# All attention-times-V matmuls of a unit in one block of a slot, in a hand-ordered cross-attention kernel

## The chip, the cores and the metric

The kernel runs on one NeuronCore of a Trainium2 chip, in one launch. The metric is the device time of that launch in microseconds, the median of the runs shown. Five engines run their own instruction streams and meet only at semaphores: TensorE (PE; its weight loads are shown as PEld), VectorE (DVE), ScalarE (ACT), GpSimd (POOL) and SyncE (SP), which here issues all DMAs.

## The reference

Cross attention with 16 heads of width 32, a residual and a layer norm, for 8 batches of 224 queries (width 512) over 750 context tokens:

```
q = x @ Wq.T + bq; k = ctx @ Wk.T + bk; v = ctx @ Wv.T + bv      # 16 heads of 32
att = softmax(q k^T / sqrt(32)); o = att v; o = o @ Wo.T + bo
y = layernorm(x + o, eps=1e-5) * gamma + beta
```

## The kernel before, in words

**Units, steps, slots.** Four heads form a unit, so a batch has 4 units and the launch has 32 (`NU`). The whole order is written out by hand. A batch is 32 steps, in 4 groups of 8 (`UNIT`). Each engine walks the same steps in its own loop and has its own list of what is due in each. Batches 0, 6 and 7 and a last, shorter iteration 8 are written out; batches 1 to 5 are a hardware loop (`batches`, line 265).

**What a step holds.** In step s of group g TensorE first does the query-major scores of the next step's head and half of the queries: 2 matmuls of 375 keys (`scores`, line 491). VectorE takes the row maxima of them (`row_max`, line 744). They are only there to find each query's maximum; their three half banks are used in turn (`RING = 3`), and the last half of a batch is put into bank 1 (`BANK[-1] = 1`, line 73). The unit before (u−1) has its maxima turned by TensorE to the other layout in step 0 of the group (`turn_maxima`, line 504), ScalarE copies them into the operand stack (`save_maxima`, line 637), and from step 2 on each step does two pieces of key-major scores, 2 matmuls each, into two banks in turn (`scores_keymajor`, line 514), and ScalarE's exp of each (`exp`, line 644). The exps give `probsT`, keys by queries, 6 key tiles of 125 keys.

**Attend and sums.** `attend(u, g, k, batch)` (line 530) multiplies key tile k of `probsT` with V for the four heads of a unit: 4 float32 matmuls, each in its own 32 columns of the array (the trace shows 8 records). `sum_keys` (line 558) does the same with ones on `head_sums`, which POOL has added up over the key tiles, 3 instructions a head (`sum_head`, line 854). Both write `ps_attn`. After the sums ScalarE copies `ps_attn` out (`copy_attn`), VectorE inverts the sums in two halves and scales (`invert_sums`, `scale_attn`), and ScalarE and VectorE save a high and a low float16 part (`attn_high`, `attn_low`). `STAGES` (line 100) gives for each of these how many groups behind the unit's scores it comes, and in which step of that group; `due` reads it, `TAIL` is the same for iteration 8.

**Tasks.** At the end of a step TensorE may have one task: K, Q or V projections (12 matmuls each, 3 for each product of float16 parts), transposes of context or x (4), or half of the output projection O (12). They go in turn into the two banks of `ps_task`. ScalarE saves the high part one step later, then VectorE the low part (`save_task`, line 701; V has only the VectorE copy). The next task but one waits for that save (line 609). `OWN`, `NEXT` and `OUTPUT` (lines 89 to 94) say which task is in which step, for this batch, the next, and the one before.

**SyncE's order.** In each batch: fill the stacks of unit 2 (16 DMAs), move V tiles 0 to 3 from `v_next` to `v_now`, fill the stacks of unit 3, move V tiles 4 and 5, load the next inputs, fill the stacks of unit 0 of the next batch, store the outputs, load the residual, fill those of unit 1. A move may start only when the last attend with the old tile is done. In the written-out batches it waits for that attend itself; in the loop it waits for the save of the first task at or after step `LAST_USE + k` (line 399). The first unit of a batch waits for the moved tile k in its attend k (line 536).

Of the kernel before, what the change touches and what calls it, by code (L numbers as in the profile page):

```python
# [15 lines left out]
def build(nc, x, ctx_tokens, Wq, bq, Wk, bk, Wv, bv, Wo, bo, gamma, beta, out):  # L50
# [7 lines left out]
    KT = 6  # L58
# [4 lines left out]
    UNIT = 2 * HG  # L63
# [13 lines left out]
    NU = B * UNITS  # L77
# [11 lines left out]
    OWN = {0: ("K", 2, 0), 1: ("V", 0), 2: ("K", 2, 1), 3: ("Q", 2), 4: ("K", 3, 0), 5: ("V", 1), 8: ("K", 3, 1),  # L89
           9: ("V", 2), 11: ("V", 3), 12: ("Q", 3), 14: ("V", 4), 17: ("V", 5)}  # L90
    NEXT = {6: ("ctxT", 0), 10: ("ctxT", 1), 13: ("ctxT", 2), 15: ("K", 0, 0), 16: ("K", 1, 0), 18: ("ctxT", 3),
            19: ("ctxT", 4), 20: ("xT", 0), 21: ("ctxT", 5), 22: ("xT", 1), 23: ("K", 0, 1), 25: ("Q", 0),
            27: ("K", 1, 1), 29: ("Q", 1)}
    OUTPUT = {24: ("O", 0), 26: ("O", 1)}
    assert all(len(t) % 2 == 0 for t in (OWN, NEXT, OUTPUT))
    assert not OWN.keys() & NEXT.keys() and not (OWN.keys() | NEXT.keys()) & OUTPUT.keys()
    O_STEPS = sorted(OUTPUT)


    STAGES = {**{("attend", k): (2, 2 + k) for k in range(KT)}, "sum_keys": (2, 7), "copy": (3, 0), ("invert", 0): (3, 1),  # L100
              ("invert", 1): (3, 2), "scale": (3, 3), "high": (3, 4), "low": (3, 5)}
    TAIL = {NU - 3: {"copy": 0, ("invert", 0): 1, ("invert", 1): 2, "scale": 3, "high": 4, "low": 5},
            NU - 2: {**{("attend", k): max(k, 1) for k in range(KT)}, "sum_keys": 5, "copy": 6, ("invert", 0): 7, ("invert", 1): 8,
# [5 lines left out]
    assert 2 * UNIT + LOW_STEP < O_STEPS[0] and O_STEPS[1] < 3 * UNIT + HIGH_STEP  # L109
    LAST_USE = UNIT + 2  # L110
# [63 lines left out]
    with ExitStack() as stack:  # L174
# [151 lines left out]
        def _(sp):  # L326
# [50 lines left out]
            def iteration(b):  # L377
# [9 lines left out]
                if 0 in tasks:  # L387
# [4 lines left out]
                    def move(k):  # L392


                        if isinstance(b, int):
                            need(sp, attn_ready, KT * (UNITS * b - 1) + k + 1)
                            sp.wait_ge(task_saved, after(("V", k)))
                        else:
                            s = min(s for s in tasks if s >= max(STEP_OF["V", k], LAST_USE + k))
                            sp.wait_ge(task_saved, before + tasks[s][1] + 1)  # L400
                        move_v(k)
# [37 lines left out]
        def _(pe):  # L439
# [144 lines left out]
            def iteration(b):  # L584
                tasks = iteration_tasks(b)
                before = tasks_before(b)
                for s in range(STEPS):
# [4 lines left out]
                    if u is not None:  # L592
                        if s % UNIT == 0:
                            turn_maxima(u, (g - 1) % UNITS)
# [30 lines left out]
        def _(act):  # L625
# [47 lines left out]
            def iteration(b):  # L673
                tasks = iteration_tasks(b)
                before = tasks_before(b)
                for s in range(STEPS):
# [7 lines left out]
                    if u is not None:  # L684
                        if s % UNIT == 0:
                            save_maxima(u, (g - 1) % UNITS)
# [246 lines left out]
```

## Time and profile before

| | us |
|---|---|
| three runs | 739.58, 738.58, 736.05 |
| median | 738.58 |
| span of the profiled execution, first to last instruction | 737.1 |
| PE, PEld busy | 688.3, 441.4 |
| DVE, ACT, POOL busy | 515.8, 336.3, 454.9 |
| mean granted TensorE clock | 0.980 |

For the profiled execution there is only its span; no time outside it was recorded. Matmuls are pipelined and their records overlap, so the cost of a group of them is the distance from its start to the start of the next. In a timeline a row is: start, us, engine, line, operation, names, shapes, how many merged, and in brackets the idle time before it and what ended it. Times count from the span's start.

### The profile page before, as it was taken

To read this page: it belongs to the slowest core of one execution; us is meant where nothing else is said; L and a number is where in the kernel's file an instruction comes from. 1 tells how busy PE (TensorE), PEld (TensorE's weight loads), DVE (VectorE), ACT (ScalarE), POOL (GpSimd) and SP (SyncE) were. 2 spreads that over 40 slices of the span, in tenths; PEclk is the share of its full clock that TensorE was granted. 3 is DMA by queue.
4 is the path that set the end of the run, shared out by engine and by line. 5 is a ranking of instruction groups with operands and counts; after the bars stand their busy time and mean duration, and the time that the engine had idled before them with its cause. 6 is when DMAs were issued, how large, how long until landed. Compare 5 with 4: busy or idle time off the path is not lost.

```text
span 737.1 us, 16224 instructions
## 1 busy us (share of the span) xinstructions
PE 688.3 (93%) x5496; PEld 441.4 (60%) x5496; DVE 515.8 (70%) x967; ACT 336.3 (46%) x657; POOL 454.9 (62%) x458
## 2 busy tenths in 40 slices
PE   5849999999999999999999999999999999999884
PEld 4626765666656665666656665666656666566542
DVE  2626676668867588777776688666886677666796
ACT  3501464546444464445444464444545464344461
POOL 9200666665686567674587666764686756776763
PEclk8979999999999999999999999999999999999998
DMA  4843233222332332323323223323323321223110
GB/s 156 268 123 87 88 108 103 58 69 75 123 82 61 95 110 79 88 67 87 125 78 74 83 92 101 85 57 94 113 68 93 97 57 27 83 66 93 32 52 26
DMA packets 46867, 64.95 MB, mean 88 GB/s; under 512 B 14781, under 2 KB 27069, under 8 KB 46829
## 3 DMA queue, kind: packets, MB, share of 16 engines
q1 hardware_dynamic: 46829, 64.45, 30.5%
q8 instruction: 23, 0.38, 0.2%
q14 instruction: 15, 0.12, 0.1%
HBM read 24.52 MB, written 3.67 MB: 38 GB/s over the span
## 4 chain that ended last, share of the span: by engine, by line
PE 81%; DVE 8%; DMA 6%; issue 4%; SPq 1%; DVEq 0%; ACT 0%; POOL 0%
PE ps_task L487 36%; PE ps_attn L539 10%; PE ps_scores L500 10%; PE ps_scoresT L525 8%; PE ps_task L448 6%; DVE top_halves L749 4%; PE ps_task L461 3%; DMA ctx_in<-in_ctx 3%; DMA stacks<-parts 2%; PE ps_scoresT L509 2%; PE ps_attn L565 2%; PE ps_task L465 1%; DVE y L734 1%; DVE attn_parts L779 1%; DMA v_now<-v_next 1%
## 5 line engine op out<-in xcount | busy, mean ns | idle before, releaser
L749 DVE TENSOR_REDUCE top_halves<-ps_scores 112x1 f32<-112x375 f32 x512 | 253.8, 537 | 191.9 <-PE ps_scores L500 190.8
L859 POOL TENSOR_TENSOR pair_sums<-probsT 125x672 f32<-125x672 f32 x122 | 201.2, 1650 | 209.2 <-ACT probsT L651 203.3
L651 ACT ACTIVATE probsT<-ps_scoresT 125x448 f32<-125x448 f32 x384 | 187.9, 541 | 183.9 <-PE ps_scoresT L525 181.5
L500 PE MATMUL ps_scores<-stacks 96*112 96x375 f16 x512 | 131.1, 333 | 23.7 <-DMA stacks<-parts 11.8
L487 PE MATMUL ps_task<-wvT,ctxT 128*125 128x512 f16 x576 | 133.3, 381 | 0.0
L487 PE MATMUL ps_task<-ctxT,wkT 128*128 128x375 f16 x744 | 131.1, 326 | 0.0
L539 PE MATMUL ps_attn<-probsT,v_now 125*32 125x224 f32 x1488 | 109.8, 367 | 1.3 <-DMA v_now<-v_next 1.2
L525 PE MATMUL ps_scoresT<-stacks 100*125 100x224 f16 x768 | 106.8, 260 | 0.3 <-ACT stacks L640 0.2
L487 PEld LDWEIGHTS ps_task<-wvT,ctxT 128*125 128x125 f16 x576 | 76.6, 136 | 47.2 <-issue 7.5
L487 PEld LDWEIGHTS ps_task<-ctxT,wkT 128*128 128x128 f16 x744 | 68.6, 98 | 56.8 <-issue 18.4
L500 PEld LDWEIGHTS ps_scores<-stacks 96*112 96x112 f16 x512 | 62.2, 131 | 61.4 <-DVE top_halves L749 24.7
L525 PEld LDWEIGHTS ps_scoresT<-stacks 100*125 100x125 f16 x768 | 88.9, 136 | 13.3 <-ACT probsT L651 2.9
L864 POOL TENSOR_TENSOR head_sums<-pair_sums 125x224 f32<-125x224 f32 x122 | 81.7, 669 | 10.1
L867 POOL TENSOR_TENSOR head_sums<-head_sums,pair_sums 125x224 f32<-125x224 f32 x122 | 82.0, 672 | 9.6
L633 ACT ACTIVATE parts<-ps_task,bk 128x375 f16<-128x375 f32 x62 | 35.6, 575 | 109.6 <-PE ps_task L487 109.6
L762 DVE RECIPROCAL recip<-attn_sums 128x112 f32<-128x112 f32 x64 | 53.5, 840 | 1.5 <-ACT attn_sums L659 1.5
L539 PEld LDWEIGHTS ps_attn<-probsT,v_now 125*32 125x32 f32 x1488 | 29.7, 108 | 28.6 <-DMA v_now<-v_next 1.7
L448 PE MATMUL ps_task<-woT,attn_parts 128*112 128x512 f16 x192 | 44.5, 382 | 0.1
L487 PE MATMUL ps_task<-xT,wqT 128*128 128x224 f16 x384 | 42.2, 259 | 0.0
L487 PEld LDWEIGHTS ps_task<-xT,wqT 128*128 128x128 f16 x384 | 35.2, 98 | 8.4 <-issue 5.4
L711 DVE SCALAR_TENSOR_TENSOR parts<-ps_task,bk,parts 128x375 f16<-128x375 f32 x62 | 37.0, 597 | 1.7 <-ACT parts L633 1.7
L448 PEld LDWEIGHTS ps_task<-woT,attn_parts 128*112 128x112 f16 x192 | 23.7, 130 | 18.3 <-issue 4.0
(87 smaller groups left out, 588.1 us busy)
## 6 DMA issues: line engine op xcount, KB each, us to landing
stacks<-parts SPq DMA_DIRECT2D x256, 60.9 KB, 2.0
v_now<-v_next SPq DMA_DIRECT2D x48, 250.0 KB
ctx_in<-in_ctx SPq DMA_DIRECT2D x7, 1500.0 KB
stacks<-parts SPq DMA_DIRECT2D x128, 46.9 KB, 2.0
x_in<-in_x SPq DMA_DIRECT2D x8, 448.0 KB, 14.8
resid<-in_x SPq DMA_DIRECT2D x8, 448.0 KB, 4.2
out_y<-y SPq DMA_DIRECT2D x16, 224.0 KB, 2.3
stacks<-parts SPq DMA_DIRECT2D x128, 14.0 KB, 1.8
```

The costliest lines, as they stand in the source:

```text
L448: last = nc.tensor.matmul(bank[0:QP, :], attn_parts[:, a, k, QP * q:QP * q + QP], wT["o"][:, c, k, :], start=(k == 0 and (a, c) == (0, 0)) ...
L487: last = nc.tensor.matmul(dst, lhsT, rhs, start=first, stop=(n_mm == 0))
L500: nc.tensor.matmul(ps_scores[0:QP, BANK[i], 0:KH], stacks[0:STACK_ROWS, g, h, NK + QP * q:NK + QP * q + QP], stacks[0:STACK_ROWS, g, h, KH ...
L525: last = nc.tensor.matmul(ps_scoresT[0:KP, piece % 2, NQ * i:NQ * i + NQ], stacks[:, g, h, KP * k:KP * k + KP], stacks[:, g, h, Qc], start ...
L539: last = nc.tensor.matmul(ps_attn[c:c + DK, 0:NQ], v_now[0:KP, k, P * g + c:P * g + c + DK], probsT[0:KP, g % 2, h, k, :], start=(k == 0), ...
L651: nc.scalar.activation(probsT[0:KP, g % 2, h, 2 * j:2 * j + 2, :].rearrange("p k q -> p (k q)"), ps_scoresT[0:KP, piece % 2, 0:2 * NQ], AC ...
L711: nc.vector.scalar_tensor_tensor(dst, src, b16, high, ALU.add, ALU.subtract).then_inc(task_saved, 1)
L749: nc.vector.tensor_reduce(top_halves[0:QP, g % 2, q, h, c:c + 1], ps_scores[0:QP, BANK[2 * s + c], 0:KH], AX.X, ALU.max).then_inc(half_top ...
L762: nc.vector.reciprocal(recip[:, cols], attn_sums[:, 1, cols]).then_inc(recip_ready, 1)
L859: nc.gpsimd.tensor_tensor(pair_sums[0:KP], probsT[0:KP, g % 2, h, 0:3, :], probsT[0:KP, g % 2, h, 3:6, :], ALU.add).then_inc(pair_sums_rea ...
L864: nc.gpsimd.tensor_tensor(head_sums[0:KP, g % 2, h, :], pair_sums[0:KP, 0], pair_sums[0:KP, 1], ALU.add).then_inc(two_sums_ready, 1)
L867: nc.gpsimd.tensor_tensor(head_sums[0:KP, g % 2, h, :], head_sums[0:KP, g % 2, h, :], pair_sums[0:KP, 2], ALU.add).then_inc(head_sums_read ...
```

## The change

All six attends and the sums of a unit move into step 1 of the group (`VISIT = 1`), two groups behind the unit's scores, and the following stages into the rest of the same group. The turn of the next unit's maxima moves from step 0 to step 1, ahead of them. Tasks are put into other steps; their number is the same. On SyncE, the loop's wait of the V moves follows the last use, which is now the same step for every key tile.

```diff
-    OWN = {0: ("K", 2, 0), 1: ("V", 0), 2: ("K", 2, 1), 3: ("Q", 2), 4: ("K", 3, 0), 5: ("V", 1), 8: ("K", 3, 1),
-           9: ("V", 2), 11: ("V", 3), 12: ("Q", 3), 14: ("V", 4), 17: ("V", 5)}
-    NEXT = {6: ("ctxT", 0), 10: ("ctxT", 1), 13: ("ctxT", 2), 15: ("K", 0, 0), 16: ("K", 1, 0), 18: ("ctxT", 3),
-            19: ("ctxT", 4), 20: ("xT", 0), 21: ("ctxT", 5), 22: ("xT", 1), 23: ("K", 0, 1), 25: ("Q", 0),
+    OWN = {0: ("K", 2, 0), 1: ("Q", 2), 2: ("K", 2, 1), 3: ("V", 0), 4: ("K", 3, 0), 5: ("V", 1), 6: ("V", 2), 7: ("V", 3),
+           8: ("K", 3, 1), 9: ("Q", 3), 10: ("V", 4), 11: ("V", 5)}
+    NEXT = {12: ("ctxT", 0), 13: ("ctxT", 1), 14: ("ctxT", 2), 15: ("xT", 0), 16: ("K", 0, 0), 17: ("ctxT", 3),
+            18: ("K", 1, 0), 19: ("ctxT", 4), 22: ("ctxT", 5), 23: ("xT", 1), 24: ("K", 0, 1), 25: ("Q", 0),
             27: ("K", 1, 1), 29: ("Q", 1)}
-    OUTPUT = {24: ("O", 0), 26: ("O", 1)}
+    OUTPUT = {20: ("O", 0), 21: ("O", 1)}
...
-    STAGES = {**{("attend", k): (2, 2 + k) for k in range(KT)}, "sum_keys": (2, 7), "copy": (3, 0), ("invert", 0): (3, 1),
-              ("invert", 1): (3, 2), "scale": (3, 3), "high": (3, 4), "low": (3, 5)}
-    TAIL = {NU - 3: {"copy": 0, ("invert", 0): 1, ("invert", 1): 2, "scale": 3, "high": 4, "low": 5},
-            NU - 2: {**{("attend", k): max(k, 1) for k in range(KT)}, "sum_keys": 5, "copy": 6, ("invert", 0): 7, ("invert", 1): 8,
+    VISIT = 1
+    STAGES = {**{("attend", k): (2, VISIT) for k in range(KT)}, "sum_keys": (2, VISIT), "copy": (2, 2), ("invert", 0): (2, 3),
+              ("invert", 1): (2, 4), "scale": (2, 5), "high": (2, 6), "low": (2, 7)}
+    TAIL = {NU - 2: {**{("attend", k): max(k, 1) for k in range(KT)}, "sum_keys": 5, "copy": 6, ("invert", 0): 7, ("invert", 1): 8,
                      "scale": 9, "high": 10, "low": 10},
...
-    LAST_USE = UNIT + 2
+    LAST_USE = UNIT + VISIT
...
-                            s = min(s for s in tasks if s >= max(STEP_OF["V", k], LAST_USE + k))
+                            s = min(s for s in tasks if s >= max(STEP_OF["V", k], LAST_USE))
...
-                        if s % UNIT == 0:
+                        if s % UNIT == VISIT:
                             turn_maxima(u, (g - 1) % UNITS)
...
-                        if s % UNIT == 0:
+                        if s % UNIT == VISIT:
                             save_maxima(u, (g - 1) % UNITS)
```

## Rows read from the trace of the kernel before

**Rows 1.** Windows, one loop batch: PE, PEld, DVE, ACT, POOL busy, clock, DMA.
```profile
290.70:375.50 84.80, 83.34 (x677) 53.30 (x673) 62.31 (x118) 40.77 (x80) 56.60 (x59) 1.00 0.31 88
```
**Rows 2.** Waits in that window: who waited for whom, us, times, longest.
```profile
PE ps_scores L500 <- DVE top_halves L749: 1.5, 1, 1.5
```
**Rows 3.** Timeline of PE, batch 3, group 0: score pairs that begin steps.
```profile
299.68 0.49 PE L500 MATMUL ps_scores<-stacks 96*112 96x375 f16 x2
...
302.16 0.49 PE L500 MATMUL ps_scores<-stacks 96*112 96x375 f16 x2
...
305.40 0.49 PE L500 MATMUL ps_scores<-stacks 96*112 96x375 f16 x2
...
309.36 0.49 PE L500 MATMUL ps_scores<-stacks 96*112 96x375 f16 x2
```
**Rows 4.** Timeline of PE, batch 0, group 1, where no attends are due yet.
```profile
78.13 0.49 PE L500 MATMUL ps_scores<-stacks 96*112 96x375 f16 x2
...
80.00 0.49 PE L500 MATMUL ps_scores<-stacks 96*112 96x375 f16 x2
...
81.13 0.49 PE L500 MATMUL ps_scores<-stacks 96*112 96x375 f16 x2
```
**Rows 5.** Timeline of PE in the tail: attends and sums in a row.
```profile
714.87 0.58 PE L539 MATMUL ps_attn<-probsT,v_now 125*32 125x224 f32 x8
715.27 0.56 PE L565 MATMUL ps_attn<-head_sums,ones 125*32 125x224 f32 x8
...
716.53 0.31 PE L525 MATMUL ps_scoresT<-stacks 100*125 100x224 f16 x1
```
**Rows 6.** Timeline of PE around a turn of maxima.
```profile
354.68 0.49 PE L500 MATMUL ps_scores<-stacks 96*112 96x375 f16 x2
355.10 0.55 PE L509 MATMUL ps_scoresT<-ident,top 112*4 112x112 f32 x4
355.58 2.80 PE L448 MATMUL ps_task<-woT,attn_parts 128*112 128x512 f16 x12
```
**Rows 7.** Timeline of DVE in batch 3.
```profile
305.77 1.00 DVE L749 TENSOR_REDUCE top_halves<-ps_scores 112x1 f32<-112x375 f32 x2 [1.50 <-PE ps_scores L500]
...
343.28 0.68 DVE L717 COPY v_next<-ps_task 125x512 f32<-125x512 f32 x1
343.88 0.84 DVE L762 RECIPROCAL recip<-attn_sums 128x112 f32<-128x112 f32 x1
344.64 0.93 DVE L749 TENSOR_REDUCE top_halves<-ps_scores 112x1 f32<-112x375 f32 x2
345.49 0.67 DVE L713 TENSOR_TENSOR ctxT<-ps_task,ctxT 128x500 f16<-128x500 f32 x1
346.07 1.03 DVE L769 TENSOR_TENSOR attn<-attn_sums,recip 128x224 f32<-128x224 f32 x1
```
**Rows 8.** Timeline of ACT: two exps of one step.
```profile
367.61 0.98 ACT L651 ACTIVATE probsT<-ps_scoresT 125x448 f32<-125x448 f32 x2
```
**Rows 9.** Timeline of SP's issues: two DMAs into stacks, two V moves.
```profile
364.21 1.22 SPq L343 DMA_DIRECT2D stacks<-parts  x2
...
681.59 1.61 SPq L349 DMA_DIRECT2D v_now<-v_next  x2
```
**Rows 10.** The chain's last V move (start, us), and the attend behind it (PE timeline).
```profile
682.46 6.42 DMA v_now<-v_next
...
688.92 0.59 PE L539 MATMUL ps_attn<-probsT,v_now 125*32 125x224 f32 x8 [1.18 <-DMA v_now<-v_next]
```
**Rows 11.** Timeline of POOL: two heads' sums begin; a beta pass.
```profile
348.50 1.64 POOL L859 TENSOR_TENSOR pair_sums<-probsT 125x672 f32<-125x672 f32 x1
...
351.80 1.64 POOL L859 TENSOR_TENSOR pair_sums<-probsT 125x672 f32<-125x672 f32 x1
...
374.12 1.28 POOL L887 TENSOR_TENSOR y<-y,beta_row 112x512 f32<-112x512 f32 x1
```
**Rows 12.** Windows, just behind the idle at the end of batch 4.
```profile
459.00:462.00 3.00, 3.00 (x24) 1.14 (x23) 1.25 (x4) 1.51 (x3) 3.00 (x3) 0.53 0.24 72
```

More of the change, by code:

```diff
@@ L108, in build @@
     SUM_STEPS = ((1, 4, 0), (1, 5, 1), (1, 7, 2), (2, 0, 3))
-    assert 2 * UNIT + LOW_STEP < O_STEPS[0] and O_STEPS[1] < 3 * UNIT + HIGH_STEP
-    LAST_USE = UNIT + 2
+    assert UNIT + LOW_STEP < O_STEPS[0] and O_STEPS[1] < 2 * UNIT + HIGH_STEP
+    LAST_USE = UNIT + VISIT
     STEP_OF = {t: s for s, t in {**OWN, **NEXT, **OUTPUT}.items()}
```

## The prediction

> **What bounds the kernel now.** I read four views. The windows row of one batch in the loop (the fourth, 84.80 us long) says which engine is full: TensorE 83.34 us busy, VectorE 62.31, POOL 56.60, ScalarE 40.77, at a granted clock of 1.00 [rows 1]. Waits in that window: TensorE idles once, 1.5 us, for a row maximum [rows 2]. So a batch is TensorE's own stream, and a TensorE microsecond saved is real until something else is late. The timelines then give prices: TensorE's by start-to-start distances, since recorded matmuls overlap.
>
> **Prices of a step on TensorE.** Between two score pairs: a Q step takes 2.48, a K step 3.24, a V step 3.96 [rows 3]. Batch 0, group 1 has no attends yet: there the Q step takes 1.87 and a context transpose step 1.13 (80.00 to 81.13) [rows 4], against 1.80 for the latter with an attend. So one lone attend costs 0.61 to 0.67, 0.64 on average, though its 8 recorded matmuls in a row need 0.38. Bare parts: scores 0.33, two key tiles 0.38, and the task: K 1.92, V 2.59, Q 1.16, O 2.64, transpose 0.44.
>
> **What the block saves.** The tail shows column-tiled groups back to back: 714.87, 715.27, then two more, and the next full-array load at 716.53 [rows 5]. Hence first 0.40, each middle one (716.53 − 0.50 − 715.27) / 2 = 0.38, last with exit 0.50. Seven groups (six attends, the sums): 0.40 + 5 × 0.38 + 0.50 = 2.80. The turn costs 0.48 with its exit and 0.09 to enter (0.42 instead of 0.33) [rows 6]. Turn to attend is not in the trace. Bounds: 0 (no switch at all; less is excluded, the four columns' matmuls still take their turn) to 0.26, all that a lone attend pays for entering and leaving; I take the nearest row, the turn's own entry, 0.09. Scores + turn + block = 0.42 + 0.38 + 0.09 + 2.80 = 3.69. A unit now pays 6 × 0.64 + 0.38 + 0.57 = 4.8, afterwards 3.36: 1.4 less, 5.7 a batch.
>
> The Trainium skill, "TensorEngine Tiling (Array Packing)", Key Properties, says that changing the tiling mode, not merely the tile, drains TensorE. The lone attend's 0.23 to 0.29 beyond its 0.38 agrees. By that rule turn and attend share one mode and their 0.09 would be nothing, some 3 us over 32 units.
>
> **What the move lays bare.** Before, attends filled the light steps. Now PE's own need per step, s0 to s31, is: 2.25 | s1 4.85 | 2.63, 3.30, 2.63, 3.30 ×3 | s8 2.25 | s9 4.85 | 3.30 ×2 | s12–15 1.15 each | s16 2.25 | s17 4.15 | 2.63, 1.15, 3.35, 3.35, 1.15, 1.15 | s24 2.25 | s25 4.85 | 0.71, 2.63, 0.71, 1.87, 0.71, 0.71. Sum 77.5; the tasks and the scores are as many as before. But VectorE owes each step a pair of maxima (0.85 to 0.92), then V save 0.60, inverse half 0.76, context save 0.58, scale 1.0 [rows 7] (low part 0.4, y and its statistics 0.7 and 0.6 by the same pitch). VectorE starts its step 0.36 after TensorE's first score load (305.40 to 305.77, [rows 3, 7]). TensorE can lead by three half banks of scores and two tasks: task s waits for the save two tasks back, which ends 1.63 into VectorE's step s−1 (0.92 + 0.66 recorded + 0.05 for the signal, an estimate from such hand-overs). Walking both queues:
> - s12–s16. VectorE starts s12 at 0.36, needs 2.28 (maxima, V, inverse), 2.45 (maxima, context, scale), 1.50; in s15 the save of the third context tile is out at 0.36 + 2.28 + 2.45 + 1.50 + 1.63 = 8.2. K of s16 waits for it and takes 1.92: 10.1 instead of 6.85, +3.3.
> - s18–s24, from s18 = 0. VectorE's s21 starts 7.5 and takes 3.0 (maxima, y, statistics, scale), s22 starts with TensorE's at 10.8 and takes 2.35 (maxima, mean, y, statistics). s23's transpose waits for that y, until 12.5. K of s24 needs the last context save, out in VectorE's s23 at 10.8 + 2.35 + 0.92 + 0.17 + 0.66 + 0.05 = 15.0, and ends at 16.9. Alone TensorE needs 15.0: +1.9.
> - s26–s0, from s26 = 0. ScalarE has Q's high part (0.4), the copy (0.45) and two exps (a pair 0.98, [rows 8]); the second ends near 2.1 and frees s27's last piece, so K ends at 4.3, not 3.3. VectorE's s28 starts at 4.7 and takes 2.2 (maxima, K save 0.5, inverse), s29 1.85 (maxima, scale), s30 starts at 8.7. The bank order ends in a 1, so the second scores of s31 wait for the last reduction of VectorE's s30, 8.7 + 0.46 + 0.54 + 0.05 = 9.75; two pieces take TensorE to 10.3, and s0 with K and one more wait to 12.6 instead of 9.6: +3.0.
> These walks: 23.3 + 13.7 + 10.1 + 4.15 + 16.9 + 4.85 + 12.6 = 85.6 a batch against 84.8.
>
> **SyncE, moved past.** Loop order on SP: fill stack 2, moves of V 0 to 3, fill stack 3, moves 4 and 5. A stack DMA holds SP 0.63 with its gap (two in 1.22), so 16 are 10.1; two V moves issued at 681.59 free the waiting attend at 688.92, 7.3 later, the second one's flight being 6.42 [rows 9, 10]. LAST_USE becomes 9, so in loop batches moves 0–3 wait for Q of s9, which now stands behind the block: saved 1.7 after s10 begins (0.36 + 0.92 + 0.43). Then 3.3 of moves, 10.1 of stack, 7.3: V tile 5 is usable 22.4 after s10. TensorE wants it at s17 + 2.8; s17 begins 6.6 + 10.1 = 16.7 after s10, so at 19.5. Wait 2.9, inside the block, with scores, exps and everything behind it. Before, tile 5 was wanted at step 23. In straight-line batches (0, 6, 7) the moves wait for attend k itself and go out during the block: tile 5 is usable after 1.7 + 10.1 + 7.3 = 19.1. Batch 6: no wait; batch 0 (s17 at 15.0): 1.3; batch 7 (no next-batch tasks, s17 at 12.9): 3.4. Where VectorE is faster than I walk, this wait grows by as much: s17 can't finish sooner. Stack 0: Q of s25 is saved 1.6 into s26, its first head lands 4.5 later at 6.2, wanted at s31, 8.4: hidden.
>
> **POOL.** A head's sum takes 3.30 (348.50 to 351.80), a gamma or beta pass 1.27 [rows 11]. The sums matmul now comes 9 us, not 20, after the last probabilities. Steps 3 to 9 and 11 to 17: room. After s25's block POOL has 5.1 of gamma and beta first, ending 3.5 into s26; four heads end at 16.6, TensorE wants the sums at 12.6 + 3.2 = 15.8. Wait 0.8, bounds 0 to 3 (contention with VectorE). V-tasks moved forward, O moved to s20/21 and the earlier turn cost nothing: saves are hidden by the long V steps, the maxima's copy by the block.
>
> **Sum.** Loop batches 1–5: 85.6 + 2.9 + 0.8 = 89.3, less 0.3 where these waits cover one another: 89.0, +4.2 each, +21. Batch 6: +1.6. Batch 0 by the same walk (no attends in s9, transposes bound by VectorE at 1.5): +2.3 and 1.3. Batch 7: VectorE binds s12–s16, s22–s24, s26–s31, +2.6 and 3.4. Prologue and the final iteration: its attends were already two in step 1, 0. Total +32. The stall at the end of a batch [rows 2] was followed once by a stretch at clock 0.53 [rows 12] and once more by one like it, about 1 us each; where TensorE comes late there anyway I take off 2. So 737.1 + 30 = 767 for the profiled execution's span, which is 1.5 below the median of the runs, 738.6: 768.
>
> **Rivals.**
> 1. The chain over SP and V doesn't bind (V lands as early as before relative to its use); VectorE's and ScalarE's lateness alone remains: +15, 753. For it: before, V made one wait of 1.2 us only. Against: LAST_USE and the order on SP. 0.20.
> 2. On the other side, faster: the light steps cost nothing because buffers ride out VectorE's peaks. Then TensorE runs 77.5 plus the V wait, which becomes 2.9 + 3.3 = 6.2, so 83.7 in loop batches, 77.5 in batch 6: some −5.5 −7 −6 for the first and last: 720. It decides if VectorE's s12–s15 take under 1.5 a step instead of 2. For it: VectorE is idle 22 of 84.8 us [rows 1]. Against: that idle lies in V steps, and ring and banks hold 1.5 steps. 0.08.
> 3. The clock: the row with 0.53 comes right behind such an idle of 1.5 [rows 2, 12]; now there are three or four such places a batch. A window at 1.2 GHz costs about 1 us (85.7 against 84.8). Two per batch: +16, 784. For it: the V wait of 2.9 sits in a stretch already thin. Against: five stalls before, two drops. 0.17.
> 4. Gains and waits cancel: 739. 0.06.
> Forecast as written: 0.49, own range 758 to 778.
>
> The range: bounds of unknowns (turn to attend ±0.15 × 32 = 5, POOL 0 to 3 × 7, V wait ±1.5 × 7) and rivals 1 and 3: 744 to 788. Under 0.5% a measurement of this kernel can't tell from none. Faster 0.09, same 0.06, slower 0.85.
>
> **What would show it.** After: first to last matmul of a block 2.3 to 2.5 us; TensorE waiting for v_now in block of group 2, 2 to 3 us in loop batches, absent in batch 6; transposes' steps near 2 us, with TensorE's weight loads waiting for VectorE; batch near 89; score loads waiting for maxima 5 us or more a batch. Wrong would be: a batch under 84.8, no v_now wait, or blocks over 3.2 us.

## The result, and the profile after

| | before | after |
|---|---|---|
| median of four runs, us | 739.08 (736.05 to 740.12) | 807.65 (807.18 to 808.39) |
| ratio, 95% interval | | 1.0937 (1.0913 to 1.0962) |
| span of the profiled execution, us | 737.1 | 806.6 |
| mean granted TensorE clock | 0.980 | 0.929 |
| PE, PEld busy, us | 688.3, 441.4 | 704.1, 479.0 |
| DVE, ACT, POOL busy, us | 515.8, 336.3, 454.9 | 503.7, 328.2, 458.2 |

The kernel became 68.6 us slower. The prediction had 768, with a range up to 788: the sign was right, and the loss was more than twice as large.

The page of the kernel after: busy time of TensorE, the granted clock in 40 slices (tenths), and the chain that ended last, by engine.

```profile
PE 704.1 (87%) x5496; PEld 479.0 (59%) x5496; DVE 503.7 (62%) x967; ACT 328.2 (41%) x657; POOL 458.2 (57%) x458
...
PEclk8879999997999889998999989999799999998888
...
PE 56%; SPq 11%; POOL 10%; DMA 10%; DVE 7%; issue 3%; ACT 2%; POOLq 0%; DVEq 0%; ACTq 0%
```

Two things to see. The chain now runs through SyncE's issues (11%) and DMA (10%) for a fifth of the span; before, SyncE had 1% and DMA 6%. And the clock has gaps all through the loop. That is also why TensorE's busy time rose although its work did not grow: a matmul at 1.2 GHz is recorded longer.

By distances between the score pairs that begin a batch, the batches last 76.2, 97.2, 95.8, 95.6, 94.5, 96.3 and 88.2 us; before they lasted 72.3, 84.8, 84.8, 84.8, 85.7, 85.5 and 85.8. From the start of batch 7 to the end it is 114.1 against 104.7. So the five loop batches hold 53.8 of the 69.5 us by which the spans differ, batch 0 3.9, batch 6 2.4 and the end 9.4.

Batch 3 in windows, to be read against [rows 1] (columns as there), and three stretches of it:

```profile
317.80:413.40 95.60, 85.16 (x672) 57.91 (x672) 60.47 (x119) 39.58 (x81) 57.16 (x59) 0.95 0.28 78
371.80:375.20 3.40, 0.59 (x8) 0.16 (x8) 0.00 (x0) 0.00 (x0) 0.00 (x0) 0.93 0.31 110
374.80:378.80 4.00, 2.54 (x20) 1.49 (x21) 0.00 (x0) 0.00 (x0) 0.00 (x0) 0.50 0.04 15
378.00:382.00 4.00, 4.00 (x18) 2.93 (x19) 1.59 (x3) 1.99 (x4) 0.00 (x0) 0.55 0.00 0
```

In the second row no engine but TensorE works, and it for 0.59 us, while DMA moves data: everything waits for one transfer. In the third and fourth it works again, but at a clock of 0.50 and 0.55, the lower level (1.2 GHz) for most of 7 us.

Around step 24 the clock falls again in four of the five loop batches. Batch 3, batch 4, and batch 3 of run 1 (below), each in a window with the same two idles, 0.65 us for maxima and 0.82 for a context save:

```profile
394.00:399.00 5.00, 3.94 (x14) 2.00 (x15) 5.00 (x11) 0.58 (x2) 4.69 (x7) 0.66 0.32 119
489.00:494.00 5.00, 3.53 (x32) 2.00 (x34) 4.86 (x12) 1.85 (x4) 4.77 (x6) 1.00 0.29 105
361.00:366.00 5.00, 3.93 (x45) 2.55 (x49) 5.00 (x11) 1.79 (x4) 4.69 (x7) 1.00 0.31 120
```

Waits of TensorE in the same batch, against [rows 2]:

```profile
PE ps_attn L505 <- DMA v_now<-v_next: 6.3, 2, 4.3
PE ps_task L453 <- DVE ctxT L679: 1.5, 2, 0.8
PE ps_scores L466 <- DVE top_halves L715: 1.3, 3, 0.7
PE ps_attn L531 <- POOL head_sums L833: 0.4, 1, 0.4
```

TensorE's timeline in step 17 of batch 3 shows the two waits inside the block. To be seen besides: what the idle does to the matmuls behind it. At the lower clock an attend's 8 records take 0.75 us to the next start (376.26 to 377.01), twice the 0.38 that the prediction works out from [rows 5].

```profile
367.32 0.26 PE L475 MATMUL ps_scoresT<-ident,top 112*4 112x112 f32 x1
367.34 0.39 PE L505 MATMUL ps_attn<-probsT,v_now 125*32 125x224 f32 x3
...
373.67 0.59 PE L505 MATMUL ps_attn<-probsT,v_now 125*32 125x224 f32 x8 [4.28 <-DMA v_now<-v_next]
376.26 0.98 PE L505 MATMUL ps_attn<-probsT,v_now 125*32 125x224 f32 x8 [2.01 <-DMA v_now<-v_next]
377.01 0.97 PE L531 MATMUL ps_attn<-head_sums,ones 125*32 125x224 f32 x8
377.92 1.09 PE L427 MATMUL ps_task<-ident,ctx_in 125*128 125x125 f32 x4
```

SyncE's timeline says why V came so late: four moves, sixteen DMAs of stack 3, and only then the last two moves.

```profile
352.55 3.71 SPq L315 DMA_DIRECT2D v_now<-v_next  x4
356.30 1.22 SPq L311 DMA_DIRECT2D stacks<-parts  x1
...
358.31 2.90 SPq L309 DMA_DIRECT2D stacks<-parts  x2
...
367.59 1.23 SPq L309 DMA_DIRECT2D stacks<-parts  x2
368.94 1.64 SPq L315 DMA_DIRECT2D v_now<-v_next  x2
```

From 356.30 to 368.94 are 12.6 us; the prediction had 10.1 from the spacing in [rows 9]. One pair took 2.90 instead of 1.22, while the first four moves' data was still under way. Their packets (2048 bytes each, 125 a tile) run one tile after another: 353.96 to 356.81, 356.70 to 359.14, 359.02 to 361.11, 361.03 to 364.34, so 10.4 us for four tiles. The last two run 370.34 to 373.10 and 373.05 to 375.92, and TensorE goes on 0.57 and 0.34 behind their ends.

### The profile page after: what moved, and what is told of

Same layout as the page of the kernel before. It is cut to its first block, busy times and chain, and to the rows that moved or that the text cites. A ratio compares the mean times of both kernels' runs of the same rounds, so it can differ in the third digit from the quotient of the medians.

```text
span 806.6 us, 16214 instructions
## 1 busy us (share of the span) xinstructions
PE 704.1 (87%) x5496; PEld 479.0 (59%) x5496; DVE 503.7 (62%) x967; ACT 328.2 (41%) x657; POOL 458.2 (57%) x458
## 4 chain that ended last, share of the span: by engine, by line
PE 56%; SPq 11%; POOL 10%; DMA 10%; DVE 7%; issue 3%; ACT 2%; POOLq 0%; DVEq 0%; ACTq 0%
PE ps_task L453 28%; DMA v_now<-v_next 6%; PE ps_scores L466 6%; PE ps_attn L505 6%; PE ps_scoresT L491 6%; SPq L309 5%; POOL pair_sums L825 5%; PE ps_task L414 5%; DVE top_halves L715 3%; SPq L311 3%; SPq L312 2%; DMA ctx_in<-in_ctx 2%; POOL head_sums L830 2%; PE ps_attn L531 2%; POOL head_sums L833 2%
## 5 line engine op out<-in xcount | busy, mean ns | idle before, releaser
L466 PE MATMUL ps_scores<-stacks 96*112 96x375 f16 x512 | 140.6, 341 | 25.4 <-DVE top_halves L715 16.3
L453 PE MATMUL ps_task<-ctxT,wkT 128*128 128x375 f16 x744 | 142.8, 346 | 9.5 <-DVE ctxT L679 9.5
L505 PE MATMUL ps_attn<-probsT,v_now 125*32 125x224 f32 x1488 | 98.2, 378 | 36.9 <-DMA v_now<-v_next 36.8
L491 PE MATMUL ps_scoresT<-stacks 100*125 100x224 f16 x768 | 118.9, 271 | 2.5 <-ACT probsT L617 1.9
L453 PEld LDWEIGHTS ps_task<-ctxT,wkT 128*128 128x128 f16 x744 | 76.5, 104 | 62.0 <-DVE ctxT L679 13.3
L466 PEld LDWEIGHTS ps_scores<-stacks 96*112 96x112 f16 x512 | 67.1, 135 | 61.1 <-DVE top_halves L715 33.9
L505 PEld LDWEIGHTS ps_attn<-probsT,v_now 125*32 125x32 f32 x1488 | 59.0, 115 | 56.5 <-DMA v_now<-v_next 43.9
L833 POOL TENSOR_TENSOR head_sums<-head_sums,pair_sums 125x224 f32<-125x224 f32 x122 | 85.2, 699 | 9.6
L830 POOL TENSOR_TENSOR head_sums<-pair_sums 125x224 f32<-125x224 f32 x122 | 82.4, 675 | 10.1
L601 ACT ACTIVATE ctxT<-ps_task 128x500 f16<-128x500 f32 x45 | 27.1, 603 | 64.8 <-PE ps_task L427 64.8
L599 ACT ACTIVATE parts<-ps_task,bq 128x224 f16<-128x224 f32 x32 | 14.3, 447 | 74.9 <-PE ps_task L453 74.9
```

Of the source, the lines that this page charges most:

```text
L453: last = nc.tensor.matmul(dst, lhsT, rhs, start=first, stop=(n_mm == 0))
L466: nc.tensor.matmul(ps_scores[0:QP, BANK[i], 0:KH], stacks[0:STACK_ROWS, g, h, NK + QP * q:NK + QP * q + QP], stacks[0:STACK_ROWS, g, h, KH ...
L491: last = nc.tensor.matmul(ps_scoresT[0:KP, piece % 2, NQ * i:NQ * i + NQ], stacks[:, g, h, KP * k:KP * k + KP], stacks[:, g, h, Qc], start ...
L505: last = nc.tensor.matmul(ps_attn[c:c + DK, 0:NQ], v_now[0:KP, k, P * g + c:P * g + c + DK], probsT[0:KP, g % 2, h, k, :], start=(k == 0), ...
L599: nc.scalar.activation(dst, src, ACT.Identity, bias=b16).then_inc(high_saved, 1)
L830: nc.gpsimd.tensor_tensor(head_sums[0:KP, g % 2, h, :], pair_sums[0:KP, 0], pair_sums[0:KP, 1], ALU.add).then_inc(two_sums_ready, 1)
```

## The experiments

Theory A: V tiles 4 and 5 stand behind stack 3 on SyncE and are wanted early now; this wait and the half clock behind it are most of the loss. Theory B: the merging itself, or the tasks' new places with VectorE late in light steps, is most of it. All ran beside the kernel before, whose median on each chip was 738.5 to 740.0.

| run | median, us | ratio to before, 95% | loop batch, us |
|---|---|---|---|
| 1 after, all moves first | 748.63 | 1.0126 (1.0108 to 1.0144) | 85.4 |
| 2 after, idle filled | 795.36 | 1.0741 (1.0701 to 1.0780) | 92.2 |
| 3 before's tasks, block in step 7 | 805.57 | 1.0907 (1.0866 to 1.0948) | 95.5 |
| 4 before's attends, after's tasks | 774.53 | 1.0490 (1.0465 to 1.0515) | 88.7 |
| 5 before, all moves first | 749.18 | 1.0117 (1.0066 to 1.0168) | 86.0 |
| 6 as 4, all moves first | 746.59 | 1.0103 (1.0076 to 1.0131) | 86.4 |
| 7 tasks dealt out again | 787.24 | 1.0648 (1.0616 to 1.0680) | 93.8 |
| 8 after, moves split in two | 768.61 | 1.0398 (1.0371 to 1.0424) | 88.3 to 92.7 |
| 9 as 7, stack 0 before the loads | 792.47 | 1.0723 (1.0702 to 1.0744) | 94.7 |
| 10 as 9, layer norm later | 801.00 | 1.0841 (1.0815 to 1.0867) | 96.2 |
| 11 as 7, loads last | 757.95 | 1.0268 (1.0244 to 1.0291) | 88.0 |
| 12 as 11, moves split | 723.15 | 0.9782 (0.9756 to 0.9808) | 81.5 |

The last column is batch 3 of the profiled execution (batches 3 and 4 for run 8). Runs 1, 5 and 6 lie within 2% of before. Run 12 is faster than before beyond its interval, though whether by 2% the interval leaves open.

### 1. After, with all six moves ahead of stack 3

```diff
-                    for k in range(4):
+                    for k in range(KT):
                         move(k)
                     fill(3)
-                    for k in range(4, KT):
-                        move(k)
```

> The changed kernel, with SyncE's order alone altered: all six V moves before the filling of stack 3. Theory A (the excess over my forecast is the wait of 6.3 us for V tiles 4 and 5 in step 17 of batches 1 to 5 and the half clock that it brings, about 2.7 us): both go, batches 1 to 5 fall from 95.6 to 86 to 87 us, the time to 752 to 760, TensorE's wait for v_now from 36.8 us to under 5. Rival B (thin steps alone pull the clock down, whatever V does): the wait goes but the half-clock windows in and behind step 17 stay, time 765 to 775. Rival C (DMA bandwidth, not the order of issue): the wait stays above 20 us, time over 795.

Measured: 748.63. Batch 3 of it in windows, and TensorE's waits in it:

```profile
293.80:379.30 85.50, 80.64 (x674) 56.20 (x673) 61.01 (x120) 39.72 (x81) 57.07 (x59) 1.00 0.31 87
```

```profile
PE ps_scores L464 <- DVE top_halves L713: 1.8, 3, 0.8
PE ps_task L451 <- DVE ctxT L677: 1.5, 2, 0.8
PE ps_attn L529 <- POOL head_sums L831: 0.6, 1, 0.6
```

No wait for V is left, the clock is 1.00, and step 17 takes 4.03 us where it took 11.89. 59.0 of the 68.6 us are the late V tiles with all that follows from them. Of the other 10.0 us in the spans (747.1 against 737.1), 3.0 have come up by the start of batch 7, 6.3 lie in batch 7 and 0.7 behind it. Batch 7 in windows, first of run 1, then of before:

```profile
635.40:713.20 77.80, 71.73 (x559) 47.05 (x557) 51.46 (x99) 30.82 (x62) 51.59 (x53) 0.91 0.25 68
```

```profile
632.40:703.90 71.50, 67.91 (x536) 41.09 (x532) 49.90 (x97) 31.52 (x62) 49.95 (x53) 0.99 0.24 66
```

With no tasks for a next batch its steps are bare. From its start to the end TensorE waits for maxima 7.1 us in 9 places against 2.2 in 3, and the clock falls to 0.91.

### 2. After, with TensorE's idle filled by matmuls

In loop batches 18 and 8 matmuls of 512 columns stand ahead of attends 4 and 5 of step 17; their result is thrown away. V lands when it did.

```diff
+                            if FILLERS[k] and g == 2 and not isinstance(b, int):
+                                place = tasks[s][1]
+                                pe.wait_ge(task_saved, before + place - 1)
+                                for _ in range(FILLERS[k]):
+                                    nc.tensor.matmul(ps_task[:, place % 2, :], wT["q"][:, 0, 0, 0:P], wT["q"][:, 0, 1, :],
+                                                     start=True, stop=True)
```

> The changed kernel, with 18 extra matmuls of 512 columns ahead of attend 4 and 8 ahead of attend 5 in step 17 of batches 1 to 5, about as long as the wait for V there; their results are thrown away. Theory A (idling is what costs clock): no window at half clock from step 17 on, the wait itself stays, batches fall from 95.6 by 2.5 to 3 us, time 792 to 796. Rival (the clock falls for the whole stretch's low load): windows stay, time 806 to 812.

Measured: 795.36, so 12.3 us come back though TensorE has more to do and V is no earlier. Windows, batch 3, and the row of attend 4:

```profile
313.90:406.10 92.20, 86.88 (x700) 58.25 (x699) 60.97 (x120) 39.67 (x81) 57.05 (x59) 1.00 0.29 81
```

```profile
370.08 0.58 PE L506 MATMUL ps_attn<-probsT,v_now 125*32 125x224 f32 x8 [0.37 <-DMA v_now<-v_next]
```

The clock stays at 1.00 in this batch, and from step 17 on in batches 2, 4 and 5. Step 18 takes 2.62 instead of 3.98, and step 24, six steps further on, 4.09 instead of 5.65. In batch 1 the matmuls fill less of the wait (2.12 us are left idle), and the clock falls there both in step 17 and around step 24. So the wait costs its own length and at least some 2.5 us a batch more by the half clock it leaves behind.

### 3. Before's tasks, the block in step 7

The tasks, `TAIL` and the turn's step are those of before, and the moves stand first as in run 1. Against the kernel after:

```diff
-    STAGES = {**{("attend", k): (2, VISIT) for k in range(KT)}, "sum_keys": (2, VISIT), "copy": (2, 2), ("invert", 0): (2, 3),
-              ("invert", 1): (2, 4), "scale": (2, 5), "high": (2, 6), "low": (2, 7)}
+    STAGES = {**{("attend", k): (2, 7) for k in range(KT)}, "sum_keys": (2, 7), "copy": (3, 0), ("invert", 0): (3, 1),
+              ("invert", 1): (3, 2), "scale": (3, 3), "high": (3, 4), "low": (3, 5)}
...
-    LAST_USE = UNIT + VISIT
+    LAST_USE = UNIT + 7
```

> The kernel before, its tasks and its turn where they were, with the six attends and the sums of a unit in one block, in step 7 of the group, and all V moves before stack 3 on SyncE. Merging saves TensorE about 1.3 us a unit by the rows (41 us in all). Theory A (light steps are then bound by VectorE and ScalarE): half or less is kept, 715 to 735. Rival (buffers ride out the peaks, merging pays in full): 697 to 705. Rival (late V again): over 739.

Measured: 805.57. That is in the third theory's range (over 739), but not by its reason: the stacks are late, not V. TensorE's waits over the run:

```profile
PE ps_scores L498 <- DMA stacks<-parts: 45.0, 10, 8.9
PE ps_scores L498 <- DVE top_halves L747: 31.4, 30, 2.8
```

Moves first, with the old tile in use until step 15, make the stacks late: in batches 1 to 5 TensorE stands 4.4 to 4.8 us at the end of step 22 for the first of stack 3. The run is inconclusive on merging, and shows that SyncE's order has no slack on the other side either.

### 4. Before's attends, one a step, with the tasks where the change puts them

Against the kernel before; `OWN` becomes that of the change.

```diff
-    NEXT = {6: ("ctxT", 0), 10: ("ctxT", 1), 13: ("ctxT", 2), 15: ("K", 0, 0), 16: ("K", 1, 0), 18: ("ctxT", 3),
-            19: ("ctxT", 4), 20: ("xT", 0), 21: ("ctxT", 5), 22: ("xT", 1), 23: ("K", 0, 1), 25: ("Q", 0),
+    NEXT = {12: ("ctxT", 0), 13: ("ctxT", 1), 14: ("ctxT", 2), 15: ("xT", 0), 16: ("K", 0, 0), 17: ("ctxT", 3),
+            18: ("K", 1, 0), 19: ("ctxT", 4), 20: ("ctxT", 5), 21: ("xT", 1), 24: ("K", 0, 1), 25: ("Q", 0),
...
-    OUTPUT = {24: ("O", 0), 26: ("O", 1)}
+    OUTPUT = {22: ("O", 0), 23: ("O", 1)}
```

> The kernel before with attends and sums as they were, one key tile a step, and only the tasks dealt out as in the changed kernel (O in steps 22 and 23, the transposes of 22 and 23 in 20 and 21, so that attention of the batch before is complete). Theory A (the placement costs only because the attends left those steps): 738 to 745. Rival (the placement itself is bad: four V steps in a row, transposes in a row): 755 or more.

Measured: 774.53. That is the rival's number, but not by its reason. TensorE's waits over the run:

```profile
PE ps_attn L539 <- DMA v_now<-v_next: 19.0, 6, 6.5
PE ps_scores L500 <- DVE top_halves L749: 17.2, 21, 1.6
```

V is late here too, in step 22. SyncE has issued the moves of V 0 to 3 4.8 us after step 13 begins, 4.5 in the kernel before, and stack 3 follows in both. But from step 13 to step 22 TensorE now takes 18.1 us, not 22.4, since two heavy tasks have left these steps. Run 6 takes the wait away.

### 5. Before, with all moves first (control)

```diff
-                    for k in range(4):
+                    for k in range(KT):
                         move(k)
                     fill(3)
-                    for k in range(4, KT):
-                        move(k)
```

> The kernel before with SyncE's order alone altered: all six V moves before stack 3. A control for the runs that carry this order. Theory A: before, V is moved a tile ahead of its use and stack 3 is wanted only at step 23, so nothing changes, 737 to 742. Rival: stack 3 then comes late (it waits for V 5 of step 17 in this order), over 755.

Measured: 749.18. TensorE's largest wait:

```profile
PE ps_scores L498 <- DMA stacks<-parts: 21.8, 6, 7.5
```

It was 11.8 in two waits before. The stack that is late is not stack 3, as the rival had it, but stack 0 of the next batch, which SyncE issues behind stack 3 and the loads: at the end of step 30 TensorE waits for it 7.3 us in batch 0 (1.5 before), and 2.5, 2.4 and 1.7 us in batches 1, 3 and 5. Of the 10.2 us between the two spans 7.9 lie in batch 0. So the order moves, stack, moves was worth 9 us to the kernel before: moving V early made something else late. With the block, V is the transfer that is wanted first.

### 6. As run 4, with all moves first

```diff
                     fill(2)
-                    for k in range(4):
+                    for k in range(KT):
                         move(k)
                     fill(3)
-                    for k in range(4, KT):
-                        move(k)
```

> One key tile a step as before, tasks dealt out as in the changed kernel (as in the run of the tasks alone, 774.5), and all V moves before stack 3. Theory A: of those 35 us nearly all is late V, since the light steps 12 to 21 leave SyncE too little time; 742 to 752. Then merging, by the difference to the changed kernel with the same order on SyncE (748.6), is worth about nothing with these tasks. Rival (the tasks' order itself costs): over 760.

Measured: 746.59. Batch 3 in windows, and its only wait on TensorE:

```profile
290.80:377.20 86.40, 83.90 (x676) 53.28 (x672) 64.23 (x118) 41.09 (x81) 56.45 (x59) 1.00 0.31 86
```

```profile
PE ps_scores L498 <- DVE top_halves L747: 2.5, 3, 1.3
```

Runs 1 and 6 differ in the merging, with the stages that follow it, and in the places of two transposes and of O. Spread: 86.4 a loop batch; block: 85.4. TensorE is busy 3.3 us less with the block (80.64 against 83.90), and 1.0 of it reaches the time; batch 0 gives 5.0 back (74.5 against 69.5), and over the launch the block is 2.0 slower, a difference that the two intervals do not separate. With these tasks merging is worth nothing that can be measured; that light steps end when VectorE does is the likely reason, argued from the walks and not tested by itself.

### 7. Tasks dealt out by VectorE's load

From run 1: the block's steps carry few or no tasks, V and K are spread over steps 2 to 15, transposes and O over steps that hold no other VectorE work.

```diff
+    OWN = {0: ("K", 2, 0), 2: ("Q", 2), 3: ("V", 0), 4: ("K", 2, 1), 5: ("V", 1), 6: ("Q", 3), 7: ("V", 2), 8: ("V", 3),
+           11: ("V", 4), 12: ("V", 5), 13: ("K", 3, 0), 15: ("K", 3, 1)}
+    NEXT = {9: ("xT", 0), 14: ("ctxT", 0), 16: ("ctxT", 1), 17: ("ctxT", 2), 18: ("xT", 1), 20: ("K", 0, 0), 22: ("K", 1, 0),
+            23: ("ctxT", 3), 24: ("ctxT", 4), 25: ("ctxT", 5), 26: ("Q", 0), 27: ("K", 0, 1), 28: ("K", 1, 1), 30: ("Q", 1)}
+    OUTPUT = {19: ("O", 0), 21: ("O", 1)}
```

> The block kept in step 1, V moves before stack 3, tasks dealt out by VectorE's load: none or a transpose in the steps of the block, K, V and O in the steps with VectorE's inverses, scale and low parts, Q and transposes between them. Theory A (what is lost beside late V is VectorE's lateness in light steps): TensorE's own 77 us a batch plus 3 to 5, so 705 to 722. Rival (lateness comes wherever there is no attend beside the exps, however tasks lie): 740 to 750.

Measured: 787.24. More than the whole loss is one wait a batch, of 8.2 to 9.5 us in batches 0 to 5, at the end of step 30 (the seventh, 8.9 us, is in the prologue):

```profile
PE ps_scores L463 <- DMA stacks<-parts: 62.4, 7, 9.5
```

SyncE's timeline shows what stack 0 stands behind (the second row is the load of x, issued behind 1.5 MB of context):

```profile
388.63 0.30 SPq L293 DMA_DIRECT2D ctx_in<-in_ctx  x1
389.18 5.44 SPq L296 DMA_DIRECT2D x_in<-in_x  x1
394.73 1.18 SPq L310 DMA_DIRECT2D stacks<-parts  x1
```

### 8. After, each V move in two DMAs, of 112 and 13 partitions

The waits for a moved tile count two DMAs instead of one.

```diff
-                sp.dma_start(v_now[0:KP, k], v_next[0:KP, k]).then_inc(v_moved[k], DMA)
+                for rows_of_v in (slice(0, 112), slice(112, KP)):
+                    sp.dma_start(v_now[rows_of_v, k], v_next[rows_of_v, k]).then_inc(v_moved[k], DMA)
```

> The changed kernel with each V move split into two DMAs, of 112 and 13 partitions instead of 125, same order on SyncE. In the trace a move of 125 partitions flows for 2.6 us, and moves queue one behind the other. Theory A (a count that 16 divides is spread over more DMA engines): 112 partitions flow in 1 us or less, SyncE's stall of 2 us while it issues stack 3 goes, the wait in step 17 falls from 6.3 to 3 to 5, and with it some half-clock windows: 780 to 800. Rival (the flow is bound by bytes or by the read side): each half as slow per byte, and more issues: 807 to 825.

Measured: 768.61, 39 us better than after with SyncE's order unchanged. TensorE's timeline at attends 4 and 5 of step 17 of batch 4:

```profile
447.18 0.59 PE L506 MATMUL ps_attn<-probsT,v_now 125*32 125x224 f32 x8 [1.79 <-DMA v_now<-v_next]
448.67 0.59 PE L506 MATMUL ps_attn<-probsT,v_now 125*32 125x224 f32 x8 [0.91 <-DMA v_now<-v_next]
```

SyncE's timeline, the last DMAs of stack 3 and the last moves; and a window over the first of these:

```profile
443.05 1.23 SPq L309 DMA_DIRECT2D stacks<-parts  x2
444.39 2.88 SPq L316 DMA_DIRECT2D v_now<-v_next  x4
```

```profile
445.40:446.90 1.50, 0.00 (x0) 0.00 (x0) 0.00 (x0) 0.00 (x0) 0.00 (x0) 1.00 0.54 171
```

The packets of a tile now pass in 1.2 us, where they took 2.6, and one tile follows another after 1.4 to 1.5, the time that SyncE needs to issue two DMAs. Stack 3 is issued in 10.2 us (434.24 to 444.39), the spacing of [rows 9], without the stall. The mean share of the 16 DMA engines is 0.54 here, and 0.31 in the window of after in which V alone flows: 0.31 of 16 is 5, 0.54 is more than 8.

The Trainium skill, "DMA: Bandwidth & Descriptors", "Why a DMA increments its semaphore by 16 and not by 1", says that a DMA is put on the largest number of engines up to 16 that divides the slowest dimension of both its sides, which is here the partitions. That makes 5 for 125, 16 for 112 and 13 for 13. The share of 0.31 agrees with the 5; the 0.54 is a mean over both parts and the gaps between them and shows only that they ran on more than 5.

Loop batches come in two lengths here. Batches 3 and 4 in windows:

```profile
301.10:393.80 92.70, 85.62 (x673) 58.07 (x672) 60.68 (x120) 39.77 (x81) 57.40 (x59) 0.94 0.28 80
393.80:482.10 88.30, 80.95 (x672) 55.90 (x672) 60.72 (x118) 39.39 (x81) 56.83 (x59) 1.00 0.30 85
```

The same program, the same work, the same idles for V within 0.03 us, 4.4 us apart by the clock alone: steps 17, 18 and 24 take 8.30, 4.34 and 5.77 us in batch 3, and 7.14, 2.62 and 4.09 in batch 4.

### 9. As run 7, stack 0 issued before the loads of context and x

The loads' own waits, for the transposes that still read the old inputs, go with it; they now stand behind the wait of stack 0.

```diff
+                    sp.wait_ge(task_saved, after(("K", 0, 0), ("K", 0, 1), ("Q", 0)))
+                    fill_stack(0)
...
                         load_ctx(b + 2)
...
                         load_x(b + 2)
-                    sp.wait_ge(task_saved, after(("K", 0, 0), ("K", 0, 1), ("Q", 0)))
-                    fill_stack(0)
```

> The new order of tasks (787.2) with one more move on SyncE: stack 0 of the next batch before the loads of context and x of the batch after it. There TensorE stood 11 us in step 30 of each batch for stack 0, which SyncE issued behind the 5.4 us of the x load, its data behind 1.5 MB of context. Theory A (SyncE's order alone spoiled the new order): step 30 falls from 12 to 3 us, a batch from 93.8 to 82 to 84.5, the time to 718 to 732, below the kernel before. Rival (stack 0 is late because its last K is projected in step 27, whatever the loads do): over 745.

Measured: 792.47; the wait moved instead of going. Step 30 falls from 12.14 to 2.49, step 6 rises from 1.86 to 11.87, and TensorE waits there for stack 1. The chain of waits gives the reason: the store of the output, issued behind the loads, holds SyncE until it has landed.

```profile
318.09 0.36 SPq L317
...
318.71 10.56 DMA out_y<-y
```

### 10. As run 9, the layer norm's last steps one step later

```diff
-                    wait_for_rstd = 4 if last else 3
+                    wait_for_rstd = 4
...
-                            if s == O_STEPS[q] + 2:
+                            if s == O_STEPS[q] + 3:
                                 rstd_of(q, b - 1)
...
-                            if s == O_STEPS[q] + 4:
+                            if s == O_STEPS[q] + 5:
                                 times_gamma(q, b - 1)
-                            if s == O_STEPS[q] + 5:
+                            if s == O_STEPS[q] + 6:
                                 plus_beta(q, b - 1)
```

> The same with the layer norm's steps on POOL and VectorE (rstd, centering, gamma, beta) one step later, so that POOL doesn't stand before a mean with head sums queued behind it. Theory A (POOL's head sums are late at the block of step 25 by about 1.2 us a batch for that reason): 5 to 9 us less than the run before it. Rival (POOL is late by the sum of its own work): the same within 2 us.

Measured: 801.00, 8.5 us worse. The relief itself came: TensorE's wait for `head_sums` falls from 8.4 us in 7 places to 0.2 in 1. But VectorE's maxima became late instead (`top_halves` waits 19.8 in 20 places against 7.1 in 14), and the mean clock fell from 0.941 to 0.929. So theory A had the cause of POOL's lateness right and the gain wrong.

### 11. As run 7, both loads behind stack 1

```diff
-                    if not (isinstance(b, int) and b == LAST - 1):
-                        sp.wait_ge(task_ready, after(*[("ctxT", i) for i in range(KT)]))
-                        load_ctx(b + 2)
-                        sp.wait_ge(task_ready, after(("xT", 0), ("xT", 1)))
-                        load_x(b + 2)
                     sp.wait_ge(task_saved, after(("K", 0, 0), ("K", 0, 1), ("Q", 0)))
                     fill_stack(0)
...
                     fill_stack(1)
+                    if not (isinstance(b, int) and b == LAST - 1):
+                        load_x(b + 2)
+                        load_ctx(b + 2)
```

> The new order of tasks, SyncE's order now by due time: stack 0, the stores, the residual, stack 1, and only then the loads of x and of context. The run before had lost the 11 us of step 30 and found them again in step 6: stack 1 stood behind the 5.4 us of the x load and behind a store whose landing, 11 us after its issue, waited for the context's data. Theory A (only SyncE's order): no wait for a stack over 2 us, a batch of 82 to 85, time 718 to 735. Rival (SyncE and the DMA queues are full in a batch this short, so that the wait only moves again, now to x and context): over 750.

Measured: 757.95. TensorE's waits over the run:

```profile
PE ps_attn L500 <- DMA v_now<-v_next: 24.6, 18, 2.0
PE ps_scores L461 <- DMA stacks<-parts: 8.6, 2, 8.3
```

No stack is late in the loop any more (8.3 of the 8.6 are in the prologue), but V is again.

### 12. Run 11 with the split moves of run 8

```diff
-                sp.dma_start(v_now[0:KP, k], v_next[0:KP, k]).then_inc(v_moved[k], DMA)
+                for rows_of_v in (slice(0, 112), slice(112, KP)):
+                    sp.dma_start(v_now[rows_of_v, k], v_next[rows_of_v, k]).then_inc(v_moved[k], DMA)
```

> The run before it (758.0) with each V move split into DMAs of 112 and 13 partitions. What is left there in step 17 of batches 1 to 6 is late V again, 24.6 us in all, with a half-clock window behind it; the rest of such a batch comes to about 82 us against 84.8 to 85.8 of the kernel before. Theory A (V's flow is the last thing in the way): the wait under 5 us in all, a batch of 81.5 to 83, time 716 to 726, the first version below the kernel before. Rival (six more issues on SyncE push a stack or the loads past their time): over 740.

Measured over six runs: 723.15 (720.51 to 726.6), before on the same chip 739.11, ratio 0.9782 (0.9756 to 0.9808). It is faster than both kernels. The gain lies in the loop batches; from the start of batch 7 to the end it takes 107.7 us, 3.0 more than before. Batch 3 in windows, and TensorE's waits in it:

```profile
284.10:365.60 81.50, 79.04 (x675) 56.68 (x673) 59.40 (x119) 40.20 (x81) 56.70 (x59) 1.00 0.32 91
```

```profile
PE ps_attn L527 <- POOL head_sums L829: 0.9, 1, 0.9
PE ps_task L423 <- DVE parts L673: 0.6, 1, 0.6
PE ps_scores L462 <- DVE top_halves L711: 0.4, 1, 0.4
```

A loop batch is 3.3 us shorter than in [rows 1] and 4.0 longer than the 77.5 that TensorE's own steps sum to in the prediction. Nothing waits for V in it, and TensorE is busy 79.04 of 81.50.

## Why the prediction was right and wrong, point by point

- **Sign and place: right.** TensorE waits for `v_now` inside step 17's block in every loop batch, for the reason given: SyncE's order and `LAST_USE`. In batch 6, where a move waits for the attend itself, step 17 takes 5.77 instead of 11.89; the prediction had no wait there, the trace has 1.5.
- **The walks over TensorE, VectorE and ScalarE: right in their sums.** They gave 85.6 for a loop batch without the V wait, 86.4 with POOL's 0.8; run 1, which has no V wait, takes 85.4. Part by part, walk against run 1: steps 1 to 7 23.3 and 24.0, 8 to 11 13.7 and 13.6, 12 to 16 10.1 and 9.5, 18 to 24 16.9 and 17.2, 26 to 0 12.6 and 12.4. Rival 1 had 753 for this case, and run 1 measured 748.6. Single signs were off: TensorE stood 1.3 us a batch for maxima and its weight loads 3.5, not 5 or more; the transposes' steps 12 to 15 took 1.14, 1.36, 2.20 and 1.75, not near 2 each.
- **The block: right, slightly dear.** Scores, turn, block and two key tiles' scores take 3.55 us (step 9: 4.71 less Q's 1.16), predicted 3.69. From the block's first record's start to its last's are 2.83, predicted 2.3 to 2.5: its first attends share their time with the turn. Turn and attends run into each other: in step 17 the turn's first record starts at 367.32 and the first attends at 367.34, so of the 0 to 0.26 bound for the change between them 0 was right. The Trainium skill, "TensorEngine Tiling (Array Packing)", Key Properties, says that a change of the tiling mode, and not of the tile alone, drains TensorE. The trace agrees with it here, and by it the prediction's estimate would have been 3 us lower.
- **POOL: right.** One wait of 0.4 to 0.7 a batch in step 1, predicted 0.8.
- **The step that failed: "Then 3.3 of moves, 10.1 of stack, 7.3 ... Wait 2.9".** They measured 3.75 (352.55 to 356.30), 12.6 and, to the second attend, 7.3 (368.94 to 376.26), and the wait 6.3. The chain was right, its middle term wrong by 2.5: I priced an issue by an undisturbed row and left out that SyncE stalls while four V tiles, 2.6 us each, drain ahead of it. Run 8 bears this out: with the tiles split, the same 16 issues take 10.2. Step 17 also began 0.6 earlier than the walk said, and the wait is measured from there. 2.9 + 0.45 of moves + 2.5 + 0.6 is 6.45; the trace has 6.3.
- **The second that failed: the clock.** I took 1 us for a window at 1.2 GHz from two loop batches, took 2 us off for the clock in the sum, and made its loss a rival with two such windows, by itself, instead of a consequence of the wait. (The prediction's five stalls with two drops are six at the ends of batches 1 to 6, with two drops.) After waits of 4.28 and 2.01 the clock stays low until about 382, and falls again in step 24 beside idles of 0.65 and 0.82; the windows of the result show that the same idles brought no fall in batch 4 or in run 1, so these idles alone do not decide it. Filling the idle in run 2 brought back 3.4 us in batches 2 and 3 and 12.3 over the launch. Rival 3's mechanism and mine were not alternatives: both held at once.
- **The sum of a loop batch.** Predicted 89.3 less 0.3, measured 95.6. Step 17 is 4.8 over (11.89 against 4.15 + 2.9), steps 18 to 24 3.2 over (20.1 against 16.9), all the rest 1.7 under.
- **The written-out batches.** Batch 0 +3.9 (predicted 3.6), batch 6 +2.4 (1.6), from batch 7 on +9.4 (6.0); there step 17 took 9.68 us, again for V.
- **Rival 2, faster.** The light steps do cost: the walks held. But run 12 shows that a kernel with the block can be faster, when tasks follow VectorE's load and transfers the order in which they are wanted. The same task order and SyncE order without the block was not run, so whether merging pays at all there, and how much of run 12's 16 us is the merging and how much the order, stays open. The nearest pair, runs 1 and 6, gives the block 1.0 us in a loop batch and nothing over the launch.

Of the 68.6 us, then: 59.0 are V tiles 4 and 5 behind stack 3 (run 1), at least 12.3 of these by the clock that the wait pulls down (run 2). The 9.6 that are left lie for the most part in batch 7 (6.3 of 10.0 in run 1's span, at a mean clock of 0.91). I put them down to VectorE's lateness beyond what the block saves, with its own loss of clock; that is argued from the waits for maxima, and these parts were not taken apart.

## What to carry to other kernels

Work that is gathered into one block takes its inputs all at once: for each of them, redo the sum from the release of the buffer over the issuing queue to its landing, against the block's start, and order the queue by when things are now wanted. Price an issuing queue with the data already in flight ahead of it, and a long wait of TensorE with the half clock that can follow it. TensorE time saved counts only in steps that another engine doesn't already end; here that is what the walks and run 1's waits suggest.

## What the runs showed of the hardware that I had not expected

- A move of a 125-partition tile within SBUF flows for 2.6 us at a DMA share of 0.31, and such moves go one behind another; split into 112 and 13 partitions it flows for 1.2, one tile every 1.4 to 1.5. The split alone was worth 39 us (run 8) and 35 us (from run 11 to 12).
- SyncE's issue of a pair of DMAs rose from 1.22 to 2.90 us when earlier ones' data was under way. An x load's issue took 4.36 us behind a context load in the kernel before, and 5.44 in run 7. A store issued behind these loads took 10.56 to land.
- One kernel's batches ran at 88.3 or 92.7 us by the clock alone, with the same idles. Idles of 0.65 and 0.82 us came with a stretch at the lower level in four of after's five loop batches, but in none of run 1's, which has no V wait, and in none of batches 2 to 5 of run 2, where that wait is filled.
